# Two input copies moved behind the state's high and low parts in a pipelined slot

## The chip, the core and the metric

The kernel runs on one core of a Trainium2 chip. Its engines are PE (TensorE, matrix multiplication), ACT (ScalarE), DVE (VectorE), POOL (GpSimd) and SP (SyncE, which issues DMAs here). They run side by side, each in its own program order, and wait for each other through semaphores. The metric is the device time of one execution in microseconds (us); the figure for a kernel is the median of its runs.

## The reference

For 64 batch rows, 128 channels and 2048 positions the reference applies an S4D layer: a masked causal convolution with a kernel that is a sum of 64 complex exponentials, a direct term, and the residual.

```python
dt = jnp.exp(log_dt)
A = -jnp.exp(log_A_real) + 1j * A_imag
dtA = A * dt[:, None]
Cs = Cc * (jnp.exp(dtA) - 1.0) / A
K = 2.0 * jnp.einsum('hn,hnl->hl', Cs, jnp.exp(dtA[:, :, None] * arange(L))).real
...
u_m = u * mask[:, None, :]                    # positions below the row's length
y = irfft(rfft(u_m, n=2L) * rfft(K, n=2L))[..., :L] + u_m * D[:, None]
out = x + y * mask[:, None, :]
```

## The kernel before

The convolution is computed in chunks of 256 positions. Inside a chunk it is a product with a Toeplitz matrix; between chunks it goes through a state of 64 complex numbers (128 partitions), which is carried from chunk to chunk by powers of the exponentials (`RV`). Every operand of a wide product is kept as a high part and a low part (`uhi`/`ulo`, `uoh`/`uol`, `ehi`/`elo`, `zhi`/`zlo`, `fhi`/`flo`, `thi`/`tlo`), and `three` (L1108) multiplies them in three matmuls: high by high, low by high, high by low. ACT makes the high parts by copies, DVE and POOL the low parts by a subtraction.

One **slot** is one channel. Slots 0 to 11 and 120 to 127 are written out; the 108 between them run in a hardware loop of 18 rounds of six (`groups`). A slot of channel h works on several channels at once: `here` is h, `one` is h+1, `two` is h+2 and `back` is h-1. Each engine has a `slot` function that fixes the order of its own work; nothing else orders it.

- PE (slot, L1185): `even_sums(one)` and `odd_sums(one)` write the chunk sums of channel h+1 into the PSUM bank `v` (six matmuls of 448 columns); `turn_x(two)` transposes the input of channel h+2 into `xt_even` and `xt_odd`; `toep_even`, `toep_odd` and `turn_e(two)` follow; last comes `from_state(here)`, which multiplies `zhi` and `zlo` into the outputs `y`. `even_sums` waits for `uhi`, `elo` and `ulo`, `odd_sums` for `uod` and `uol`, and `from_state` for `flo` and `zlo`.
- ACT (slot, L735): `x_odd_high(one)` copies `xt_odd` to `uoh`; `t_high(here)`, `f_high(one)` (which waits until `from_state` of h-1 is done); `turn_evens(here)` and `turn_odds(one)`, two half copies each from `v` to the buffer `room`, `turn_odds` after the signal of `odd_sums`; `x_high(two)` makes `uhi`, `x_odd(two)` copies `xt_odd` to `uod`; `z_high(here)` scales `v` into `zhi` once `odds(here)` has ended; `turn_pairs(one)`, `e_high(two)`.
- DVE (slot, L1025): two `choose(back)` put the masked result into `xall`; `odds_turned(here)`, `pairs_turned(one)`, `odds(here)`, `pairs(one)` are steps of the state scan on `mid` and `v`; `x_low(two)` makes `ulo`, `z_low(here)` makes `zlo`; `fours_turned(one)`, `e_low(two)` (`elo`), `fours(one)`, `sixth(one)`.
- POOL (slot, L560): `product`, `f_low(here)`, `odd_low(one)` (`uol`, a subtraction of 448 columns, after `uod` and `uoh`), `product`, `t_low(here)`, `difference(two)`.
- SP loads `x` three channels ahead, stores the result of h-1, and loads the Toeplitz rows.

Line 585 is the copy helper of ACT, 780 the subtraction helper of DVE, 968 the scan helper of DVE; which call a record belongs to is told by its tiles and its place. The buffers `turned` and one of the three `uod` buffers lie in the tile `room`, so those copies are listed under that name.

Of the kernel before, what the change touches and what calls it, by code (L numbers as in the profile page):

```python
# [49 lines left out]
def s4d_kernel(nc, x, length, log_dt, C, log_A_real, A_imag, D, out):  # L50
    ctx = ExitStack()
    with ctx:
# [211 lines left out]
        def e_bank(j):  # L264

            return yb[(j + 1) % 2][1][:, 0:2 * P]

        def on(g, j, d):

            return g + (j + d) // SLOTS, (j + d) % SLOTS  # L270

        def chan(g, j):
            return g * SLOTS + j
# [5 lines left out]
        def exists(g, j, d):  # L279

            return not isinstance(g, int) or 0 <= chan(g, j) + d < H
# [301 lines left out]
        def _(act):  # L583
            def copy(dst, src):
                return act.activation(dst, src, ACT.Copy)  # L585

            def x_high(g, j):
                act.wait_ge(s_tr, 2 * chan(g, j) + 1)
                copy(uhi[j % 3][:], xt[0][:]).then_inc(s_uhi, 1)

            def x_odd(g, j):
                act.wait_ge(s_tr, 2 * chan(g, j) + 2)
                copy(uod[j % 3][:], xt[1][:]).then_inc(s_uod, 1)

            def x_odd_high(g, j):
                act.wait_ge(s_tr, 2 * chan(g, j) + 2)
                if exists(g, j, -2):
                    act.wait_ge(s_in, chan(g, j) - 1)
                copy(uoh[j % 2][:], xt[1][:, 0:EVERY]).then_inc(s_uoh, 1)
# [92 lines left out]
            def k_copy(k):  # L692
                act.wait_ge(s_kfill, k + 1)
                copy(*k_part(k)).then_inc(s_ksb, 1)

            def e_high(g, j):
                act.wait_ge(s_et, chan(g, j) + 1)
                copy(ehi[j % 2][:], e_bank(j)).then_inc(s_ehi, 1)

            def f_high(g, j):  # L700
                if exists(g, j, -1):
                    act.wait_ge(s_pf, chan(g, j))
                else:
                    act.wait_ge(s_pf0, 1)
                if exists(g, j, -2):
                    act.wait_ge(s_y, 2 * chan(g, j) - 2)
                copy(fhi[j % 2][:], pf[j % 2][:, ::-1]).then_inc(s_fhi, 1)

            def t_high(g, j):
                act.wait_ge(s_t[j % 2], 16 * (chan(g, 0) // 2 + j // 2 + 1))  # L710
                copy(thi[j % 2][:], traw[j % 2][:, ::-1]).then_inc(s_thi, 1)
# [6 lines left out]
            def turn_odds(g, j):  # L718
                act.wait_ge(s_in, chan(g, j) + 1)
                turned_halves(turned[j % 2][:, 0:3], chunks(vb[j % 2])[:, 1:6:2]).then_inc(s_turn1, 1)  # L720

            def turn_pairs(g, j):
                act.wait_ge(s_pairs, chan(g, j) + 1)
                turned_halves(turned[j % 2][:, 3:5], chunks(vb[j % 2])[:, 2:5:2]).then_inc(s_turn2, 1)

            def turn_evens(g, j):
                act.wait_ge(s_evens, chan(g, j) + 1)
                turned_halves(turned[j % 2][:, 0:3], chunks(vb[j % 2])[:, 2:7:2]).then_inc(s_turn4, 1)

            def z_high(g, j):  # L730
                act.wait_ge(s_states, chan(g, j) + 1)
                act.activation(zhi[j % 2][:, B:], vb[j % 2][:, B:NC * B], ACT.Copy,
                               scale=RV[:, 6:7, chan(g, j)]).then_inc(s_zhi, 1)

            def slot(g, j):  # L735
                here, one, two = (g, j), on(g, j, 1), on(g, j, 2)
                has0, has1, has2 = exists(g, j, 0), exists(g, j, 1), exists(g, j, 2)
                if has1:
                    x_odd_high(*one)
                t_high(*here)  # L740
                if has1:
                    f_high(*one)
                turn_evens(*here)
                if has1:
                    turn_odds(*one)
                    if isinstance(g, int) and g == 0 and 1 <= j <= 4:
                        k_copy(j)
                if has2:
                    x_high(*two)
                    x_odd(*two)  # L750
                z_high(*here)
                if has1:
                    turn_pairs(*one)
                if has2:
                    e_high(*two)

            e_high(0, 0)
# [13 lines left out]
        def _(dve):  # L771
# [7 lines left out]
            def less(dst, src, high):  # L779
                return dve.tensor_tensor(dst, src, high.bitcast(F32), ALU.subtract)  # L780

            def x_low(g, j):
                dve.wait_ge(s_uhi, chan(g, j) + 1)
                return less(ulo[j % 3][:], xt[0][:], uhi[j % 3][:]).then_inc(s_ulo, 1)
# [164 lines left out]
            def e_low(g, j):  # L949
                dve.wait_ge(s_ehi, chan(g, j) + 1)  # L950
                less(elo[j % 2][:], e_bank(j), ehi[j % 2][:]).then_inc(s_elo, 1)

            def choose(g, j, part):

                a = part * 512
                dve.memset(tick[:, part:part + 1], 0.0)
                dve.copy_predicated(xs[j][:, a:a + 512], mask[:, a:a + 512], yb[j % 2][part][:]).then_inc(s_pred, 1)  # L957
# [8 lines left out]
            def times(out, src, h, k, other):  # L966

                return dve.scalar_tensor_tensor(out=out, in0=src, scalar=RV[:, k:k + 1, h], in1=other,  # L968
                                                op0=ALU.mult, op1=ALU.add)

            def pairs_turned(g, j):

                h, z, m, w = scan(g, j)
                dve.wait_ge(s_turn1, h + 1)
                times(m[:], w[:, 0:3], h, 1, z[:, 2:7:2]).then_inc(s_mid1, 1)

            def pairs(g, j):

                h, z, m, w = scan(g, j)
                dve.wait_ge(s_mid1, h + 1)  # L980
                times(z[:, 2:7:2], z[:, 1:6:2], h, 0, m[:]).then_inc(s_pairs, 1)

            def scan(g, j):

                return chan(g, j), chunks(vb[j % 2]), mid[j % 2], turned[j % 2]
# [7 lines left out]
            def fours(g, j):  # L993

                h, z, m, w = scan(g, j)
                dve.wait_ge(s_mid2, h + 1)
                times(z[:, 6:3:-2], z[:, 4:1:-2], h, 2, m[:, 1::-1]).then_inc(s_fours, 1)
# [9 lines left out]
            def odds_turned(g, j):  # L1007

                h, z, m, w = scan(g, j)
                dve.wait_ge(s_turn4, h + 1)  # L1010
                times(m[:], w[:, 0:3], h, 1, z[:, 3:8:2]).then_inc(s_mid4, 1)

            def odds(g, j):

                h, z, m, w = scan(g, j)
                dve.wait_ge(s_mid4, h + 1)
                times(z[:, 3:8:2], z[:, 2:7:2], h, 0, m[:]).then_inc(s_states, 1)

            def z_low(g, j):
                dve.wait_ge(s_zhi, chan(g, j) + 1)  # L1020
                dve.scalar_tensor_tensor(out=zlo[j % 2][:, B:], in0=vb[j % 2][:, B:NC * B], scalar=RV[:, 6:7, chan(g, j)],  # L1021
                                         in1=zhi[j % 2][:, B:].bitcast(F32), op0=ALU.mult,
                                         op1=ALU.subtract).then_inc(s_zlo, 1)

            def slot(g, j):  # L1025
                h = chan(g, j)
                here, one, two, back = (g, j), on(g, j, 1), on(g, j, 2), on(g, j, -1)
                has0, has1, has2, hasb = exists(g, j, 0), exists(g, j, 1), exists(g, j, 2), exists(g, j, -1)
                if hasb:
                    dve.wait_ge(s_y, 2 * h - 1)  # L1030
                    choose(*back, 0)
                    dve.wait_ge(s_y, 2 * h)
                    choose(*back, 1)
                odds_turned(*here)
                if has1:
                    pairs_turned(*one)
                odds(*here)
                if has1:
                    pairs(*one)
                if has2:  # L1040
                    x_low(*two)
                z_low(*here)
                if has1:
                    fours_turned(*one)
                if has2:
                    e_low(*two)
                if has1:
                    fours(*one)
                    sixth(*one)
                if isinstance(g, int) and g == 0 and j == 1:  # L1050
                    dve.wait_ge(s_ksb, 1)
                    add_d(slice(1, 5))
                if isinstance(g, int) and g == 0 and j == 4:
                    dve.wait_ge(s_ksb, 4)
                    add_d(slice(5, SQ))
# [260 lines left out]
```

## Time and profile before

| | us |
|---|---|
| median of 3 runs | 862.51 (862.41 to 863.89) |
| profiled execution | 864.69 |
| its span (first to last instruction) | 862.8 |
| mean granted clock of TensorE | 0.996 of full speed |

The page gives PE as busy for 821.8 us (95% of the span), DVE 743.1, ACT 674.4 and POOL 603.6. Matmuls are pipelined, so their records overlap and a full row does not mean that PE never waits: a wait shows in the distance between the starts of its weight loads (PEld) and matmuls. In the timelines the first column is the start in us from the span's start, the second the duration; "x4" merges four records.

### The profile page before, as it was taken

What the parts mean: (1) busy time and instruction counts of PE and PEld (TensorE: products, weight loads), DVE (VectorE), ACT (ScalarE), POOL (GpSimd) and SP (SyncE); (2) the same over time, 40 slices, a digit from 0 to 9 for tenths busy, and PEclk for the clock granted to TensorE, in tenths of its full rate; (3) what the DMA queues carried; (4) which work ended last, traced back from release to release, by engine and by line L of the source; (5) the groups of instructions that cost most, each with busy time, mean ns of one, the idle gap of its engine ahead of it and who ended that gap; (6) DMA issues with size and microseconds to landing.
All of it is one profiled execution on the core that took longest, in us unless ns stands there. A gap on an engine that the chain in (4) does not pass through costs nothing.

```text
span 862.8 us, 23096 instructions
## 1 busy us (share of the span) xinstructions
PE 821.8 (95%) x6299; PEld 787.6 (91%) x6299; DVE 743.1 (86%) x2041; ACT 674.4 (78%) x1722; POOL 603.6 (70%) x847
## 2 busy tenths in 40 slices
PE   0779999999999999999999999999999999999997
PEld 0668999999999999999999999999999999999996
DVE  7857898888888888888888888888888888888886
ACT  4667887878788887878787878888787878787874
POOL 5965767667676767677776767676767777776763
PEclk9989999999999999999999999999999999999999
DMA  4133677777676776767676767677676767676764
GB/s 106 34 84 94 185 198 185 193 178 191 188 194 188 191 191 185 193 185 193 184 190 187 195 185 193 188 192 190 186 195 181 197 181 197 181 193 186 197 186 135
DMA packets 161394, 152.73 MB, mean 177 GB/s; under 512 B 13656, under 2 KB 161240, under 8 KB 161240
## 3 DMA queue, kind: packets, MB, share of 16 engines
q1 hardware_dynamic: 161064, 152.15, 65.9%
q8 instruction: 12, 0.20, 0.1%
q10 hardware_dynamic: 304, 0.26, 0.1%
q14 instruction: 14, 0.11, 0.0%
HBM read 84.02 MB, written 67.30 MB: 175 GB/s over the span
## 4 chain that ended last, share of the span: by engine, by line
PE 88%; ACT 3%; DMA 3%; DVE 3%; SPq 1%; issue 1%; POOL 0%; DVEq 0%; ACTq 0%; POOLq 0%
PE y L1110 15%; PE y L1111 13%; PE y L1112 13%; PE y L1158 12%; PE xt_even L1095 6%; PE xt_odd L1095 6%; PE v L1110 6%; PE v L1112 6%; PE v L1111 6%; DMA xall<-in_x_dram 3%; PE y L1105 2%; PE y L1106 2%; SPq L369 1%; ACT B L585 0%; DVE zlo L1021 0%
## 5 line engine op out<-in xcount | busy, mean ns | idle before, releaser
L585 ACT ACTIVATE room<-v 64x192 f32<-64x192 f32 (+1 forms) x768 | 236.4, 308 | 27.5 <-PE v L1112 2.4
L968 DVE SCALAR_TENSOR_TENSOR mid<-room,RV,v 128x192 f32<-128x192 f32 (+2 forms) x512 | 185.1, 361 | 73.8 <-ACT room L585 55.9
L557 POOL TENSOR_TENSOR uol<-uod,uoh 128x448 fp32r<-128x448 f32 x85 | 98.4, 1158 | 139.9 <-issue 139.9
L968 DVE SCALAR_TENSOR_TENSOR v<-v,RV,mid 128x192 f32<-128x192 f32 (+2 forms) x512 | 177.7, 370 | 16.5
L1110 PE MATMUL y<-thi,uhi 128*128 128x256 f32 x511 | 186.4, 365 | 0.0
L957 DVE COPY_PREDICATED xall<-mask,y 128x512 f32<-128x512 int32 x254 | 178.2, 752 | 1.4 <-issue 1.3
L538 POOL TENSOR_TENSOR room<-W,B 128x256 f32 (+1 forms) x254 | 161.8, 637 | 23.5 <-POOL room L547 11.1
L1110 PE MATMUL y<-fhi,zhi 128*128 128x256 f32 x511 | 153.7, 301 | 3.2 <-DVE zlo L1021 3.2
L1112 PE MATMUL y<-fhi,zlo 128*128 128x256 f32 x511 | 144.2, 282 | 0.0
L1111 PE MATMUL y<-tlo,uhi 128*128 128x256 f32 x511 | 144.1, 282 | 0.0
L1111 PE MATMUL y<-flo,zhi 128*128 128x256 f32 x511 | 144.1, 282 | 0.0
L1112 PE MATMUL y<-thi,ulo 128*128 128x256 f32 x511 | 143.9, 282 | 0.0
L1158 PE MATMUL y<-traw,uod 128*128 128x128 f32 x680 | 131.2, 274 | 0.0
L1110 PEld LDWEIGHTS y<-fhi,zhi 128*128 128x128 f32 x511 | 96.6, 189 | 14.6 <-issue 4.2
L1158 PEld LDWEIGHTS y<-traw,uod 128*128 128x128 f32 x680 | 105.1, 191 | 0.0
L1111 PEld LDWEIGHTS y<-tlo,uhi 128*128 128x128 f32 x511 | 98.4, 193 | 0.0
L1110 PEld LDWEIGHTS y<-thi,uhi 128*128 128x128 f32 x511 | 98.0, 192 | 0.1
L557 POOL TENSOR_TENSOR uol<-room,uoh 128x448 fp32r<-128x448 f32 x43 | 49.7, 1157 | 68.5 <-issue 68.0
L1111 PEld LDWEIGHTS y<-flo,zhi 128*128 128x128 f32 x511 | 97.1, 190 | 0.0
L1112 PEld LDWEIGHTS y<-fhi,zlo 128*128 128x128 f32 x511 | 97.0, 190 | 0.0
L528 POOL TENSOR_TENSOR tlo<-traw,thi 128x256 fp32r<-128x256 f32 x128 | 94.6, 739 | 2.9 <-ACT thi L585 2.9
L1112 PEld LDWEIGHTS y<-thi,ulo 128*128 128x128 f32 x511 | 96.5, 189 | 0.0
(223 smaller groups left out, 1987.1 us busy)
## 6 DMA issues: line engine op xcount, KB each, us to landing
xall<-in_x_dram SPq DMA_DIRECT2D x256, 256.0 KB, 4.3
out_dram<-xall SPq DMA_DIRECT2D x254, 256.0 KB, 3.4
traw<-krows SPq DMA_DIRECT2D x128, 128.0 KB, 3.0
NXY<-B SPq DMA_DIRECT2D x2, 512.0 KB, 6.3
krows<-ksb SPq DMA_DIRECT2D x8, 1.0 KB, 2.1
krows<-ksb SPq DMA_DIRECT2D x8, 4.0 KB, 3.8
krows<-ksb SPq DMA_DIRECT2D x8, 11.0 KB, 3.8
out_dram<-xall SPq DMA_DIRECT2D x1, 128.0 KB, 2.4
```

The source lines that it names most:

```text
L528: pool.tensor_tensor(tlo[j % 2][:], traw[j % 2][:, ::-1], thi[j % 2][:].bitcast(F32), ALU.subtract).then_inc(s_tlo, 1)
L538: pool.tensor_tensor((tw1, tw2)[which], w, b, ALU.mult).then_inc(s_gpa, 1)
L557: pool.tensor_tensor(uol[j % 2][:], uod[j % 3][:, 0:EVERY], uoh[j % 2][:].bitcast(F32), ALU.subtract).then_inc(s_uol, 1)
L585: return act.activation(dst, src, ACT.Copy)
L957: dve.copy_predicated(xs[j][:, a:a + 512], mask[:, a:a + 512], yb[j % 2][part][:]).then_inc(s_pred, 1)
L968: return dve.scalar_tensor_tensor(out=out, in0=src, scalar=RV[:, k:k + 1, h], in1=other, op0=ALU.mult, op1=ALU.add)
L1095: mm = pe.transpose(xt[par][:, c * P:(c + 1) * P], xs[j][:, b * BLK:(b + 1) * BLK], ident[:])
L1105: pe.transpose(e_bank(j)[:, 0:P], pf[j % 2][:, 0:P], ident[:])
L1110: pe.matmul(o, a_hi, b_hi, start=start, stop=False, skip_group_check=True)
L1111: pe.matmul(o, a_hi, b_lo, start=False, stop=False, skip_group_check=True)
L1112: return pe.matmul(o, a_lo, b_hi, start=False, stop=stop, skip_group_check=True)
L1158: mm = pe.matmul(y_cols(g, j, c)[:, BLK:2 * BLK], uod[j % 3][:, b], traw[k][:, :BLK - 1:-1], start=False, stop=False, skip_group_check=True)
```

## The change

In ACT's slot `x_odd(two)` moves from behind `x_high(two)` to behind `turn_pairs(one)`, so that `z_high(here)` stands directly behind `x_high(two)`. In DVE's slot `x_low(two)` moves from ahead of `z_low(here)` to behind `fours_turned(one)`, and `fours(one)` now stands ahead of `e_low(two)`. Nothing is added or removed, and the instructions of PE, POOL and SP stand as before.

```diff
@@ ACT slot
                 if has2:
                     x_high(*two)
-                    x_odd(*two)
                 z_high(*here)
                 if has1:
                     turn_pairs(*one)
                 if has2:
+                    x_odd(*two)
                     e_high(*two)
@@ DVE slot
                 odds(*here)
                 if has1:
                     pairs(*one)
-                if has2:
-                    x_low(*two)
                 z_low(*here)
                 if has1:
                     fours_turned(*one)
                 if has2:
+                    x_low(*two)
+                if has1:
+                    fours(*one)
+                if has2:
                     e_low(*two)
                 if has1:
-                    fours(*one)
                     sixth(*one)
```

ACT in the loop, before, from `x_high(two)` to `x_odd_high` of the next slot. ISA and REGISTER_ALU are instructions of the sequencer that set an address or a count; here one of them, and not `zhi`, carries the wait for `s_states`, the signal of `odds`.

```order
L585 ACTIVATE uhi<-xt_even 128x512 [waits s_tr]
L592 REGISTER_ALU
L585 ACTIVATE uod<-xt_odd 128x512 [waits s_tr]
L732 ISA [waits s_states]
L732 ACTIVATE zhi<-v,RV 128x448
L585 ACTIVATE room<-v 64x128 [waits s_pairs]
L585 ACTIVATE room<-v 64x128
L697 REGISTER_ALU
L585 ACTIVATE ehi<-y 128x256 [waits s_et]
L585 ACTIVATE uoh<-xt_odd 128x448 [waits s_in,s_tr]
```

The same place of ACT in the changed kernel:

```order
L585 ACTIVATE uhi<-xt_even 128x512 [waits s_tr]
L732 ISA [waits s_states]
L732 ACTIVATE zhi<-v,RV 128x448
L585 ACTIVATE room<-v 64x128 [waits s_pairs]
L585 ACTIVATE room<-v 64x128
L592 REGISTER_ALU
L585 ACTIVATE uod<-xt_odd 128x512 [waits s_tr]
L697 REGISTER_ALU
L585 ACTIVATE ehi<-y 128x256 [waits s_et]
L585 ACTIVATE uoh<-xt_odd 128x448 [waits s_in,s_tr]
```

The copy to `uod` now stands behind the wait for `s_states` and ahead of `ehi` and `uoh`, as one instruction with its register step.

DVE in the loop, before, from `odds(here)` to `fours(one)`:

```order
L968 SCALAR_TENSOR_TENSOR v<-v,RV,mid 128x3x64 [waits s_mid4]
L968 ISA [waits s_mid1]
L968 SCALAR_TENSOR_TENSOR v<-v,RV,mid 128x3x64
L783 REGISTER_ALU
L780 TENSOR_TENSOR ulo<-xt_even,uhi 128x512 [waits s_uhi]
L1021 ISA [waits s_zhi]
L1021 SCALAR_TENSOR_TENSOR zlo<-v,RV,zhi 128x448
L968 ISA [waits s_turn2]
L968 SCALAR_TENSOR_TENSOR mid<-room,RV,v 128x128
L780 TENSOR_TENSOR elo<-y,ehi 128x256 [waits s_ehi]
L968 ISA [waits s_mid2]
L968 SCALAR_TENSOR_TENSOR v<-v,RV,mid 128x2x64
```

The same place of DVE in the changed kernel:

```order
L968 SCALAR_TENSOR_TENSOR v<-v,RV,mid 128x3x64 [waits s_mid4]
L968 ISA [waits s_mid1]
L968 SCALAR_TENSOR_TENSOR v<-v,RV,mid 128x3x64
L1021 ISA [waits s_zhi]
L1021 SCALAR_TENSOR_TENSOR zlo<-v,RV,zhi 128x448
L968 ISA [waits s_turn2]
L968 SCALAR_TENSOR_TENSOR mid<-room,RV,v 128x128
L783 REGISTER_ALU
L780 TENSOR_TENSOR ulo<-xt_even,uhi 128x512 [waits s_uhi]
L968 ISA [waits s_mid2]
L968 SCALAR_TENSOR_TENSOR v<-v,RV,mid 128x2x64
L780 TENSOR_TENSOR elo<-y,ehi 128x256 [waits s_ehi]
```

`ulo` has gone behind `zlo` and `mid`, and `elo` has two instructions (`ulo` and `v`) more ahead of it since `zlo`.

## Rows read from the trace of the kernel before

**Rows 1.** Busy us (records) of PE, PEld, DVE, ACT, POOL; then PEclk, DMA share, GB/s
```profile
75.00:83.00 8.00, 7.54 (x61) 7.21 (x60) 5.98 (x16) 5.83 (x16) 4.45 (x6) 1.00 0.54 147
```

**Rows 2.** Timeline of PE's weight loads in one slot of the loop
```profile
408.95 0.30 PEld L1158 LDWEIGHTS y<-traw,room 128*128 128x128 f32 x2
409.18 0.19 PEld L1110 LDWEIGHTS y<-thi,uhi 128*128 128x128 f32 x1
...
409.53 0.31 PEld L1158 LDWEIGHTS y<-traw,room 128*128 128x128 f32 x2
409.94 0.19 PEld L1110 LDWEIGHTS y<-fhi,zhi 128*128 128x128 f32 x1
...
411.36 0.19 PEld L1110 LDWEIGHTS v<-uhi,ehi 128*128 128x128 f32 x1
...
411.89 0.19 PEld L1110 LDWEIGHTS v<-uoh,ehi 128*128 128x128 f32 x1
```

**Rows 3.** Timeline of PE in that slot: last matmul of odd_sums
```profile
406.26 0.37 PE L1112 MATMUL v<-uoh,elo 128*128 128x448 f32 x1
```

**Rows 4.** Timeline of ACT in that slot
```profile
406.67 0.33 ACT L585 ACTIVATE room<-v 64x192 f32<-64x192 f32 x1
...
407.35 0.60 ACT L585 ACTIVATE uhi<-xt_even 128x512 fp32r<-128x512 f32 x1
407.85 0.59 ACT L585 ACTIVATE uod<-xt_odd 128x512 f32<-128x512 f32 x1
408.36 0.64 ACT L732 ACTIVATE zhi<-v,RV 128x448 fp32r<-128x448 f32 x1
409.02 0.56 ACT L585 ACTIVATE room<-v 64x128 f32<-64x128 f32 x2
409.60 0.39 ACT L585 ACTIVATE ehi<-y 128x256 fp32r<-128x256 f32 x1
409.88 0.54 ACT L585 ACTIVATE uoh<-xt_odd 128x448 fp32r<-128x448 f32 x1
```

**Rows 5.** Timeline of DVE in that slot
```profile
407.47 0.41 DVE L968 SCALAR_TENSOR_TENSOR mid<-room,RV,v 128x192 f32<-128x192 f32 x1 [0.48 <-ACT room L585]
...
407.80 0.42 DVE L968 SCALAR_TENSOR_TENSOR v<-v,RV,mid 128x192 f32<-128x192 f32 x1
...
408.46 0.68 DVE L780 TENSOR_TENSOR ulo<-xt_even,uhi 128x512 fp32r<-128x512 f32 x1
409.13 0.69 DVE L1021 SCALAR_TENSOR_TENSOR zlo<-v,RV,zhi 128x448 fp32r<-128x448 f32 x1
...
410.01 0.42 DVE L780 TENSOR_TENSOR elo<-y,ehi 128x256 fp32r<-128x256 f32 x1
```

**Rows 6.** Timeline of POOL in that slot
```profile
410.55 1.16 POOL L557 TENSOR_TENSOR uol<-uod,uoh 128x448 fp32r<-128x448 f32 x1 [1.56 <-issue]
411.67 0.66 POOL L538 TENSOR_TENSOR room<-W,B 128x256 f32 x1
```

**Rows 7.** Timeline of ACT: two zhi of the loop six slots apart, two neighbours written out
```profile
302.45 0.64 ACT L732 ACTIVATE zhi<-v,RV 128x448 fp32r<-128x448 f32 x1
...
339.84 0.64 ACT L732 ACTIVATE zhi<-v,RV 128x448 fp32r<-128x448 f32 x1
...
819.42 0.64 ACT L732 ACTIVATE zhi<-v,RV 128x448 fp32r<-128x448 f32 x1
...
825.51 0.64 ACT L732 ACTIVATE zhi<-v,RV 128x448 fp32r<-128x448 f32 x1
```

**Rows 8.** Timeline of POOL in an early slot: the low part of the odd input
```profile
77.59 1.16 POOL L557 TENSOR_TENSOR uol<-room,uoh 128x448 fp32r<-128x448 f32 x1 [3.12 <-issue]
```

**Rows 9.** Timeline of PE's weight loads: two sums that started behind a wait
```profile
52.88 0.19 PEld L1110 LDWEIGHTS v<-uhi,ehi 128*128 128x128 f32 x1 [2.17 <-issue]
...
78.87 0.19 PEld L1110 LDWEIGHTS v<-uoh,ehi 128*128 128x128 f32 x1
```

**Rows 10.** Timeline of PE: third matmul of the sum whose load stands at 52.88
```profile
53.40 0.37 PE L1112 MATMUL v<-uhi,elo 128*128 128x448 f32 x1
```

## The prediction

> **What bounds the kernel now.** I read the busy times first: the page has PE at 95%, so the question is whether PE works without a break or is paced by a ring of waits. The timeline of PE's weight loads in one slot of the loop answers it. From the two loads of L1158 to the next load PE normally needs 409.18 - 408.95 = 0.23 us; ahead of the first load of `from_state` it is 409.94 - 409.53 = 0.41 [rows 2]. So PE stands still for 0.18 us in each slot, and what ends it is `zlo`: it ends at 409.13 + 0.69 = 409.82, and the load follows 0.12 later [rows 2, 5]. A slot of the loop lasts (339.84 - 302.45) / 6 = 6.232 us, one written out 825.51 - 819.42 = 6.09 [rows 7].
>
> Next I followed the ring backwards, engine by engine. `zlo` (409.13) starts 0.13 after the end of `zhi` (408.36 + 0.64 = 409.00). `zhi` starts 0.14 after the end of `odds` on DVE (407.80 + 0.42 = 408.22). `odds` stands right behind `pairs_turned` (407.47), and this one waited for ACT's `turn_odds`, which starts at 406.67, 0.04 after the last matmul of `odd_sums` (406.26 + 0.37 = 406.63) [rows 3 to 5]. So the ring is: `odd_sums` ends, `turn_odds`, `pairs_turned`, `odds`, `zhi`, `zlo`, `from_state`, the sums of the next channel. I call the start of `turn_odds` T; T is 406.67 here, and the next one is at T + 6.23.
>
> **What the change does to `zhi` and `zlo`: next to nothing in the loop.** The change takes one copy out of ACT's queue ahead of `zhi` and one subtraction out of DVE's queue ahead of `zlo`. Whether that helps depends on what each of them waited for. ACT's queue would have let `zhi` start at 407.85 + 0.50 = 408.35, taking the distance from `uhi` to `uod` (407.35 to 407.85) as the price of such a copy [rows 4]; it did start at 408.36. But the data came at 408.22, and the 0.14 after it is the distance that also stands between `zhi` and `zlo` (0.13) [rows 4, 5]; in both places an ISA instruction carries the wait. So the signal of `odds` alone already puts `zhi` at 408.36, and with `uod` out of the way it stays there. Could it come earlier? If the 0.14 were the queue's doing and the true delay were the 0.04 of `turn_odds` [rows 3, 4], `zhi` would come 0.10 earlier. I take 0 and keep 0.10 as the other end. `zlo` is the same case: `ulo` ends at 408.46 + 0.68 = 409.14, at the very moment when `zhi`'s data are usable (409.13) [rows 5]; removing `ulo` leaves `zlo` at 409.13. Gain in the loop: 0 to 0.10 us a slot, taken as 0.
>
> **What it does to the copies behind: they come half a microsecond later.** In the changed order ACT has nothing to do between the end of `uhi` and `zhi`, and pays for `uod` later. `zhi` at 408.36, the two half copies at 409.02, and at 409.60, where `ehi` stood, now `uod`. `ehi` then starts at 409.60 + 0.50 = 410.10, `uoh` at + 0.28 (409.60 to 409.88) = 410.38, and `uoh` ends at + 0.54 = 410.92 instead of 410.42 [rows 4]. That is the whole 0.50 us, and ACT is not short of time for it; what counts is who waits.
>
> POOL's `uol` waits for both copies. It started at 410.55, 0.13 after the end of `uoh`, lasts 1.16 and ended at 411.71 [rows 4, 6]; `odd_sums` loads its first weights at 411.89 [rows 2]. How soon after `uol` PE can load is in an early slot: `uol` ends at 77.59 + 1.16 = 78.75, the load stands at 78.87, 0.12 later [rows 8, 9], as after `zlo`. So the slack was 411.89 - 411.71 - 0.12 = 0.06 us, and it is asked for 0.50. **This is the term that decides.**
>
> The ring with it, in the old slot's clock: `uol` starts at 410.92 + 0.13 = 411.05 and ends at 412.21; PE loads at 412.33. When such a sum starts from a standstill its third matmul stands 53.40 - 52.88 = 0.52 behind the load [rows 9, 10]; that gives 412.85, and `turn_odds` follows 406.67 - 406.26 = 0.41 after that start [rows 3, 4]: 413.26. Less 406.67 this is a slot of 6.59 us, against 6.23: **+0.36 us**. PE now waits at `odd_sums`, some 0.4 us.
>
> **The rest of the change.** `elo`: in its old place (410.01) now stands `ulo`, which takes up to 0.67 (408.46 to 409.13), then `fours`, a scan step shorter than the 0.33 between 407.47 and 407.80, then `elo`, 0.42: it ends by 411.43 instead of 410.43 [rows 5]. `even_sums` loads at 411.36 [rows 2], so with the 0.12 it is held up by at most 0.19 us. That is hidden, because `odd_sums` behind it can't go before 412.33; without that cover it would cost 0.19. DVE has the time: it waited 0.48 us for ACT at 407.47 [rows 5], and the later `choose` and `odds_turned` use some of that. `ulo`, 1.55 us later than before, is needed only by `even_sums` too. PE's `turn_x` waits for `uod`, `uoh` and `ulo` of an earlier channel, half a slot later: nothing. POOL's `t_low` and `difference`, queued behind `uol`, slide with it, and so do the matmuls that read them, since these stand behind `odd_sums`: nothing. No DMA is moved, and SP's waits are for results that leave several slots before their buffer is loaded again.
>
> **The sum.** Loop: 108 slots x 0.36 = 38.9 us. Written out: there the wait stands on `zhi` itself, without an ISA instruction, so `zhi` may gain up to 0.10 of the 0.50; I take 0.28 us for the 12 slots of the pace of 6.09: 3.4 us. In the first five slots `uol` decides already (78.87 is its end + 0.12 [rows 8, 9]) and ACT also copies the kernel's tables ahead of `uhi`; those copies and `uoh` are not moved in time, so 0. Last two slots: neither moved call exists. In all +42 us: 864.7 + 42 = 907 for a profiled execution, 862.5 + 42 = **904.5 us** for the median, which lies 2.2 us below the profiled execution before. Both unknowns pull downwards: `zhi` 0.10 earlier makes it 108 x 0.10 = 11 us less, and if the third matmul comes 0.44 instead of 0.52 behind its load, which is my estimate where `even_sums` has only just ended, another 9. Upwards stands a tenth of the 0.36 for rounding in six links of 0.01, and any slip of POOL behind: 5 us. That makes 885 to 910.
>
> A rule speaks on POOL's part. The Trainium skill, Perfetto Trace Analysis, GPSIMD Engine Instruction, says that a GpSimd record's duration is not to be trusted and that start-to-start spacing should be used. Spacing gives 411.67 - 410.55 = 1.12 [rows 6] in place of 1.16, 120 x 0.04 = 5 us less, so 900 by the rule. The trace speaks for the record here: PE's load follows the recorded end by 0.12, as it does after DVE's `zlo` [rows 2, 5, 8, 9].
>
> **Rivals.**
> 1. *The stall goes, and nothing takes its place (faster).* It needs `odds` to be done when `uhi` frees ACT at 407.85; then `zhi` starts 0.5 earlier, `uoh` keeps its time, and PE's 0.18 us go: 120 x 0.18 = 22 us less, 841 us. Against it: `odds` ends at 408.22, and it hangs on `turn_odds`, that is on PE's own sums [rows 3 to 5]. Break-even is the point where `zhi` starts by 0.44 (0.50 less the slack of 0.06) earlier than now. 4%.
> 2. *`uoh` is late but POOL's true end lies well ahead of its record*, so that only `elo` holds up the sums: 0.06 to 0.19 us a slot, 7 to 23 us more, 870 to 885. Against it the 0.12 of [rows 8, 9]. 7%.
> 3. *The clock falls.* PE will idle more in each slot, and the Trainium skill, TensorE: Matmul & The Clock Gate, HAM oscillation, warns that repeated PE idling can bring the lower clock. In 75 to 83 us PE left 0.46 of 8 us unused and was granted 1.00 [rows 1], about what I expect now; if the loop ran at the lower clock, PE's 6.05 us a slot (6.23 - 0.18) would double, over 600 us more. 1%.
> 4. *No change*: the delay of `uoh` is absorbed, since PE has 0.18 us to give back at `from_state`. But that stall follows `zlo`, which follows the sums, so it moves with them. 3%.
>
> **How the numbers follow.** The forecast has 85%, all of it slower; rivals 2 and 3 are slower as well. The likeliest case is 904.5 us. The range is 885 to 910: the forecast's own ends, which leave out the better part of rival 2, rivals 1, 3 and 4, together 15%. Differences under 0.2% (1.7 us) can't be told from no change here. Faster 0.04, same 0.03, slower 0.93.
>
> **What would show it.** In the changed profile: slots of the loop 6.5 to 6.6 us apart; `zhi` still 0.14 behind the end of `odds` and 1.69 behind `turn_odds`; `uod` where `ehi` stood, 1.24 behind `zhi`; `uoh` ending 2.56 behind the start of `zhi` (now 2.06); `uol` named as what PE waits for at `odd_sums`, several tenths of a us in each slot; `zlo` no earlier against `turn_odds` than now (2.46). I am wrong if `zhi` starts right behind `uhi`, if `odd_sums` loads well ahead of `uol`'s recorded end, or if a slot takes 6.2 us or less.

## The result: 900.5 us, and where the time went

| | before | after |
|---|---|---|
| median | 862.56 us (862.41 to 863.89, 4 runs) | 900.49 us (900.35 to 900.62, 4 runs) |
| profiled execution | 864.7 us | 900.6 us, span 898.8 |
| one slot of the loop | 6.23 us | 6.55 us |
| one slot written out | 6.09 us | 6.34 us |

The ratio is 1.0436, with a 95% interval of 1.0418 to 1.0454: the change costs 38 us. The clock of TensorE is no part of it: the span has a mean granted clock of 0.995 (0.996 before), and the stretch of 100 us from the middle of the loop was granted the full one. The row of this stretch, after and then before (columns: start and length, busy us and instructions of PE, PEld, DVE, ACT and POOL, granted clock, DMA share, GB/s):

```profile
430.00:530.00 100.00, 98.79 (x735) 90.50 (x734) 81.03 (x229) 78.19 (x201) 66.70 (x90) 1.00 0.67 180
```

```profile
430.00:530.00 100.00, 100.00 (x772) 96.24 (x772) 87.84 (x243) 80.55 (x208) 71.75 (x97) 1.00 0.70 189
```

A warning stands in these rows too. PE's busy time fell by 1.2% (98.79 us for 100.00), the number of its matmuls by 4.8% (735 for 772). The records overlap: in PE's rows further down a matmul is recorded with 0.36 us while the next one starts 0.20 behind it, so the first 0.16 us of a standstill don't show as idle time. The distances between starts show them.

The pace of a slot comes from two `zhi` of the same kind, six slots apart: (370.24 - 330.92) / 6 = 6.55 us. Of before it was 6.23 [rows 7]. The two rows are from ACT's timeline of the changed kernel:

```profile
330.92 0.64 ACT L732 ACTIVATE zhi<-v,RV 128x448 fp32r<-128x448 f32 x1 [0.41 <-DVE v L968]
...
370.24 0.63 ACT L732 ACTIVATE zhi<-v,RV 128x448 fp32r<-128x448 f32 x1 [0.41 <-DVE v L968]
```

One slot on ACT, from one `turn_odds` to the next. In the terms of the prediction T is 434.07:

```profile
434.07 0.66 ACT L585 ACTIVATE room<-v 64x192 f32<-64x192 f32 x2 [0.45 <-PE v L1113]
434.76 0.60 ACT L585 ACTIVATE uhi<-xt_even 128x512 fp32r<-128x512 f32 x1
435.77 0.64 ACT L732 ACTIVATE zhi<-v,RV 128x448 fp32r<-128x448 f32 x1 [0.41 <-DVE v L968]
436.43 0.55 ACT L585 ACTIVATE room<-v 64x128 f32<-64x128 f32 x2
437.01 0.60 ACT L585 ACTIVATE uod<-xt_odd 128x512 f32<-128x512 f32 x1
437.50 0.38 ACT L585 ACTIVATE ehi<-y 128x256 fp32r<-128x256 f32 x1
437.76 0.55 ACT L585 ACTIVATE uoh<-xt_odd 128x448 fp32r<-128x448 f32 x1
...
440.62 0.66 ACT L585 ACTIVATE room<-v 64x192 f32<-64x192 f32 x2 [0.43 <-PE v L1113]
```

Compare with [rows 4]. There `zhi` stood 408.36 - 406.67 = 1.69 behind T, and here it stands 1.70 behind: the copy that was taken out of its way brought it nothing. The queue now has a hole of 0.41 us ahead of `zhi`, and what ends it is DVE's `v`, which is `odds`. Behind `zhi` the copy `uod` takes the place that `ehi` had, and `uoh` comes half a microsecond later.

The same slot on POOL, then PE's weight loads, then PE's matmuls. The load with `y<-fhi,zhi` is the first one of `from_state`, that with `v<-uhi,ehi` the first one of `even_sums`, and that with `v<-uoh,ehi` the first one of `odd_sums`:

```profile
438.45 1.15 POOL L557 TENSOR_TENSOR uol<-uod,uoh 128x448 fp32r<-128x448 f32 x1 [1.91 <-ACT uod L585]
```

```profile
436.95 0.30 PEld L1159 LDWEIGHTS y<-traw,uod 128*128 128x128 f32 x2
437.35 0.19 PEld L1111 LDWEIGHTS y<-fhi,zhi 128*128 128x128 f32 x1
...
438.77 0.19 PEld L1111 LDWEIGHTS v<-uhi,ehi 128*128 128x128 f32 x1
438.89 0.19 PEld L1112 LDWEIGHTS v<-ulo,ehi 128*128 128x128 f32 x1
439.09 0.19 PEld L1113 LDWEIGHTS v<-uhi,elo 128*128 128x128 f32 x1
439.71 0.19 PEld L1111 LDWEIGHTS v<-uoh,ehi 128*128 128x128 f32 x1 [0.43 <-issue]
```

```profile
439.09 0.36 PE L1112 MATMUL v<-ulo,ehi 128*128 128x448 f32 x1
439.29 0.36 PE L1113 MATMUL v<-uhi,elo 128*128 128x448 f32 x1
439.75 0.44 PE L1111 MATMUL v<-uoh,ehi 128*128 128x448 f32 x1
...
440.22 0.36 PE L1113 MATMUL v<-uoh,elo 128*128 128x448 f32 x1
```

`uoh` ends at 437.76 + 0.55 = 438.31, `uol` starts at 438.45 and ends at 439.60, and the load follows at 439.71. The profile names `uod` as what `uol` waited for, but `uod` had ended at 437.01 + 0.60 = 437.61; it is `uoh` that ended last. In the slot of before the load of `odd_sums` stood 411.89 - 411.36 = 0.53 behind that of `even_sums` [rows 2], and here 439.71 - 438.77 = 0.94, so it comes 0.41 us late.

PE's matmuls lose a little less. A load normally stands 0.20 ahead of its matmul (438.89 and 439.09), and here only 0.04 (439.71 and 439.75). What counts is the third matmul of `odd_sums`. Before, it stood here:

```profile
412.49 0.37 PE L1112 MATMUL v<-uoh,elo 128*128 128x448 f32 x1
```

That is 412.49 - 411.36 = 1.13 behind the load of `even_sums` [rows 2], and after the change 440.22 - 438.77 = 1.45. The difference, 0.32 us, is the whole growth of the slot. The old standstill ahead of `from_state` is still there: 437.35 - 436.95 = 0.40, before 0.41 [rows 2].

The view that sums up the waits of the whole span tells the same (columns: who waited at which line, for whom: us, times, longest):

```profile
PEld v L1111 <- issue: 56.2, 126, 2.2
...
ACT zhi L732 <- DVE v L968: 48.7, 122, 1.4
```

PE's loads of `v` at L1111 now wait 56.2 us in 126 places, 0.45 us each and one for nearly every channel. The profile puts this down to "issue", that is, to nothing that it sees. Only the timeline shows that the load stands 0.11 to 0.12 us behind the end of `uol`, in 126 of the 128 channels. The last row of the fence has this counterpart in the same view of the kernel before:

```profile
ACT zhi L732 <- DVE v L968: 2.2, 2, 1.4
```

From 2 waits of 2.2 us in all it went to 122 waits of 48.7 us: the queue in front of it got empty, and the data did not get any earlier.

### The profile page after: what moved, and what is told of

It is laid out like the page before. It is cut to its first block, busy times and chain, and to the rows that moved or that the text cites. A ratio compares the mean times of both kernels' runs of the same rounds, so it can differ in the third digit from the quotient of the medians.

```text
span 898.8 us, 23096 instructions
## 1 busy us (share of the span) xinstructions
PE 850.6 (95%) x6299; PEld 779.8 (87%) x6299; DVE 719.7 (80%) x2041; ACT 683.0 (76%) x1722; POOL 601.9 (67%) x847
## 4 chain that ended last, share of the span: by engine, by line
PE 88%; ACT 3%; issue 3%; DVE 2%; DMA 2%; SPq 1%; POOL 1%; DVEq 0%; ACTq 0%; POOLq 0%
PE y L1111 15%; PE y L1113 13%; PE y L1112 13%; PE y L1159 12%; PE v L1111 9%; PE xt_even L1096 6%; PE xt_odd L1096 6%; PE v L1113 5%; PE v L1112 5%; PE y L1107 1%; PE y L1106 1%; DMA xall<-in_x_dram 1%; ACT room L585 1%; POOL uol L557 1%; ACT B L585 0%
## 5 line engine op out<-in xcount | busy, mean ns | idle before, releaser
L968 DVE SCALAR_TENSOR_TENSOR mid<-room,RV,v 128x192 f32<-128x192 f32 (+2 forms) x512 | 182.5, 356 | 66.1 <-ACT room L585 66.0
L1111 PE MATMUL y<-thi,uhi 128*128 128x256 f32 x511 | 186.4, 365 | 0.0
L1111 PE MATMUL y<-fhi,zhi 128*128 128x256 f32 x511 | 153.9, 301 | 1.4 <-DVE zlo L1021 1.4
L1021 DVE SCALAR_TENSOR_TENSOR zlo<-v,RV,zhi 128x448 fp32r<-128x448 f32 x128 | 87.5, 684 | 76.5 <-ACT zhi L732 76.5
L732 ACT ACTIVATE zhi<-v,RV 128x448 fp32r<-128x448 f32 x128 | 81.2, 635 | 48.8 <-DVE v L968 48.7
L1111 PEld LDWEIGHTS y<-fhi,zhi 128*128 128x128 f32 x511 | 96.7, 189 | 12.0 <-issue 1.7
L1111 PEld LDWEIGHTS y<-thi,uhi 128*128 128x128 f32 x511 | 98.0, 192 | 0.1
```

The source lines that it names most:

```text
L1111: pe.matmul(o, a_hi, b_hi, start=start, stop=False, skip_group_check=True)
```

## The experiments

The theory is that of the prediction: the late `uoh` makes `uol` and with it `odd_sums` late, and `zhi` gains nothing from its free queue, since `odds` comes too late for it. The rivals are that DVE's half of the change does the harm (through `elo`, or through some other slip), that POOL's `uol` has nothing to do with it, and that no order of these instructions lets `zhi` go earlier.

| what was run | median us | ratio to before, 95% |
|---|---|---|
| the whole change | 900.5 | 1.042 to 1.045 |
| ACT's half alone | 900.1 | 1.042 to 1.047 |
| DVE's half alone | 864.3 | 1.001 to 1.004 |
| change, with `uoh` first | 870.0 | 1.006 to 1.011 |
| change, with `odds` first | 847.7 | 0.982 to 0.986 |
| before, with `odds` first | 861.5 | 0.998 to 1.000 |
| ACT's half, with `odds` first | 851.0 | 0.985 to 0.990 |
| change, with `odds` and `uoh` first | 843.9 | 0.976 to 0.982 |

**ACT's half alone.** Only the copy `x_odd(*two)` moves behind `z_high(*here)`; DVE's order is that of before.

```diff
 # ACT's slot
                 if has2:
                     x_high(*two)
-                    x_odd(*two)
                 z_high(*here)
 ...
                 if has2:
+                    x_odd(*two)
                     e_high(*two)
```

> ACT's half of the change alone: x_odd(two) behind turn_pairs(one); DVE as before. Theory (uoh comes 0.5 us later, and uol with it; zhi does not come earlier because it waits for the signal of odds): the same ring as in the changed kernel, a slot of the loop of 6.55 us, 899 to 902 us. Rival (DVE's half makes the loss, by holding up elo): no loss here, 858 to 864 us.

Measured: 900.13 us (898.21 to 901.13), ratio 1.0445 (1.0424 to 1.0465). This half alone costs all that the change costs. Its timelines, of ACT and then of DVE:

```profile
432.82 0.64 ACT L732 ACTIVATE zhi<-v,RV 128x448 fp32r<-128x448 f32 x1 [0.41 <-DVE v L968]
```

```profile
432.92 0.68 DVE L780 TENSOR_TENSOR ulo<-xt_even,uhi 128x512 fp32r<-128x512 f32 x1
433.60 0.68 DVE L1021 SCALAR_TENSOR_TENSOR zlo<-v,RV,zhi 128x448 fp32r<-128x448 f32 x1
```

`turn_odds` starts at 431.13 here, so `zhi` stands 1.69 behind it and `zlo` 2.47, with `ulo` still ahead of `zlo`. Both distances are those of the kernel with the whole change. Whether `ulo` stands ahead of `zlo` or not makes no difference to `zlo` as long as `odds` is late.

**DVE's half alone.** `z_low(*here)` and `fours_turned(*one)` go ahead of the subtraction that makes `ulo`; ACT's order is that of before.

```diff
 # DVE's slot
+                z_low(*here)
+                if has1:
+                    fours_turned(*one)
                 if has2:
                     x_low(*two)
-                z_low(*here)
                 if has1:
-                    fours_turned(*one)
+                    fours(*one)
                 if has2:
                     e_low(*two)
                 if has1:
-                    fours(*one)
                     sixth(*one)
```

> DVE's half alone: x_low(two) behind fours_turned(one), fours(one) ahead of e_low(two); ACT as before. Theory: zlo starts no earlier, since it waits for zhi (0.13 after its end), and elo, which in the changed kernel ended 2.12 us after zlo's start, would let even_sums load at 4.72 us behind turn_odds where it loads at 4.69 now: +0.03 us a slot, 863 to 868 us. Rival (elo holds up the sums by the upper bound of 0.19 us): 880 us or more. Rival (DVE's half alone is a gain, because ulo was in zlo's way): under 860 us.

Measured: 864.25 us, ratio 1.0025 (1.0011 to 1.0039): 1.8 us slower, so the half isn't quite free. `zhi` (432.23) stands 1.69 behind `turn_odds` (430.54), and `zlo` 2.47 behind it, though nothing is in DVE's way any more:

```profile
433.01 0.68 DVE L1021 SCALAR_TENSOR_TENSOR zlo<-v,RV,zhi 128x448 fp32r<-128x448 f32 x1 [0.59 <-ACT zhi L732]
```

DVE now waits 0.59 us with `zlo` at the head of its queue. That this costs something can be seen at `elo`, which stands behind it (DVE's timeline, then PE's loads):

```profile
428.41 0.41 DVE L780 TENSOR_TENSOR elo<-y,ehi 128x256 fp32r<-128x256 f32 x1
```

```profile
429.01 0.19 PEld L1111 LDWEIGHTS v<-uhi,ehi 128*128 128x128 f32 x1
```

The load comes 0.19 after the end of `elo` (428.82) and 429.01 - 427.50 = 1.51 behind the first load of `from_state`; undelayed it is 411.36 - 409.94 = 1.42 [rows 2]. In the next slot it is 1.42 again, 0.09 behind the end of `elo`. Over a round of six slots `zhi` stands 6.23, 6.23, 6.30, 6.27, 6.22 and 6.24 us apart, so two slots of a round are longer, and not every slot by 0.03 as I had expected. Both lie at the end of the round. The load above belongs to the last slot of PE's round. In the trace one more instruction of the sequencer (ALU_OP) stands ahead of the load there; it starts at 428.93, and the load 0.08 behind it. In the slot after it DVE's loop branches back, and `choose` starts about a third of a microsecond later than in the others; the last section has this in another kernel.

**The change, with `uoh` made earlier.** The high copy of the odd part is taken out of the start of the next slot and put right behind `uod`, ahead of `ehi`. So `uol` has back 0.26 of the 0.50 us that `uod` took from it.

```diff
 # ACT's slot
-                if has1:
-                    x_odd_high(*one)
                 t_high(*here)
 ...
                     x_odd(*two)
+                    x_odd_high(*two)
                     e_high(*two)
 # and x_odd_high(0, 1) once, ahead of the slots
```

> The changed kernel, with x_odd_high(two) moved from the start of the next ACT slot to ahead of e_high(two): uoh comes 0.26 us earlier, ehi 0.43 later. Theory (uol's arrival sets the slot): the slot shortens by that 0.26 to 6.29, unless elo, now late, takes over at about 6.35: 868 to 877 us. Rival (the loss of 38 us lies in something else than uol's arrival, such as elo): 900 us or more, since elo comes later here.

Measured: 869.99 us, ratio 1.0082 (1.0059 to 1.0106). This gives back 900.5 - 870.0 = 30.5 of the 38 us and moves nothing else by more than one copy. (`room` is the buffer of `uod` in the program's names.) In this kernel POOL and PE read:

```profile
437.48 1.16 POOL L557 TENSOR_TENSOR uol<-room,uoh 128x448 fp32r<-128x448 f32 x1 [1.74 <-ACT room L585]
```

```profile
438.75 0.19 PEld L1111 LDWEIGHTS v<-uoh,ehi 128*128 128x128 f32 x1
```

`uol` ends at 438.64 and the load stands 0.11 behind it. PE still waits for `uol`, only for less. The other part of the remaining time is `elo`, now pushed back by `uoh` on ACT (DVE's timeline, then PE's loads):

```profile
437.66 0.42 DVE L780 TENSOR_TENSOR elo<-y,ehi 128x256 fp32r<-128x256 f32 x1
```

```profile
436.65 0.19 PEld L1111 LDWEIGHTS y<-fhi,zhi 128*128 128x128 f32 x1
...
438.15 0.19 PEld L1111 LDWEIGHTS v<-uhi,ehi 128*128 128x128 f32 x1
```

`elo` ends at 438.08, when the load is just due (436.65 + 1.42 = 438.07), and the load comes 0.07 behind its end: 0.08 late. In the last slot of PE's round it is 0.19 late (`elo` ends at 431.67, the load stands at 431.86), with the same extra instruction ahead of it as with DVE's half alone. The prediction had up to 0.19 for `elo` without cover, as 0.07 for its end and 0.12 for the signal; in five slots of six it is 0.01 and 0.07. The slots are (340.22 - 302.25) / 6 = 6.33 us apart.

**The change, with `odds` made earlier.** Now the other side. The prediction's first rival (the stall goes, and nothing takes its place) needs `odds` to be done when `uhi` frees ACT. In DVE's queue `pairs_turned` of the next channel stands ahead of `odds`. Its results aren't needed by `odds`, so the two can be swapped.

```diff
 # DVE's slot
                 odds_turned(*here)
+                odds(*here)
                 if has1:
                     pairs_turned(*one)
-                odds(*here)
-                if has1:
                     pairs(*one)
```

> The changed kernel, and on DVE odds(here) stands ahead of pairs_turned(one), so that the signal zhi waits for no longer hangs on turn_odds of this slot. Theory (the only thing missing was that odds is done when uhi frees ACT): odds ends by about 0.85 us behind turn_odds, zhi starts right behind uhi (1.2 behind turn_odds instead of 1.7), uoh is back at its time of before, PE's stall ahead of from_state goes, and what is left is the ring through uoh and uol of about 6.08 us a slot: 843 to 850 us. Rival (the later copies are a loss wherever zhi stands): 890 or more. Rival (DVE becomes the bound, its scan steps now wait for each other): 860 to 880 us.

Measured: 847.68 us, ratio 0.9839 (0.9817 to 0.9860). DVE and ACT of this kernel:

```profile
433.41 0.43 DVE L968 SCALAR_TENSOR_TENSOR v<-v,RV,mid 128x192 f32<-128x192 f32 x1
...
435.06 0.68 DVE L1021 SCALAR_TENSOR_TENSOR zlo<-v,RV,zhi 128x448 fp32r<-128x448 f32 x1 [0.17 <-ACT zhi L732]
```

```profile
433.11 0.66 ACT L585 ACTIVATE room<-v 64x192 f32<-64x192 f32 x2 [0.34 <-PE v L1112]
433.79 0.60 ACT L585 ACTIVATE uhi<-xt_even 128x512 fp32r<-128x512 f32 x1
434.29 0.63 ACT L732 ACTIVATE zhi<-v,RV 128x448 fp32r<-128x448 f32 x1
```

`odds` ends at 433.84, before ACT is free, so `zhi` goes right behind `uhi`: 1.18 behind T instead of 1.70. `uod`, `ehi` and `uoh` stand behind it at the distances that they have after the change (`uoh` starts 436.28 - 434.29 = 1.99 behind `zhi`, as 437.76 - 435.77), and so the chain from T to `uol` is shorter by the 0.52. All 38 us of loss and 15 us more are gone. The load of `odd_sums` still stands 0.11 behind the end of `uol`, but in five slots of six it is in time for its matmul, which starts 0.20 behind the one before it; in the sixth it starts 0.36 behind. The mean slot, (440.35 - 403.77) / 6 = 6.10 us, is close to the 6.05 that the prediction gave PE for its own work.

**Before, with `odds` made earlier.** The same swap of DVE's two calls, in the kernel before.

> The kernel before, with only odds(here) ahead of pairs_turned(one) on DVE. Theory (zhi has two things in its way in the old kernel, the signal of odds and ACT's copy to uod, each of which alone holds it at 1.69 us behind turn_odds): taking away one of them gives next to nothing, 0.02 us a slot, 857 to 863 us. Rival (the signal of odds was the whole matter, and the change is not needed for the gain): 846 to 850 us.

Measured: 861.49 us, ratio 0.9992 (0.9980 to 1.0004): no difference. ACT in this kernel:

```profile
412.48 0.60 ACT L585 ACTIVATE uhi<-xt_even 128x512 fp32r<-128x512 f32 x1
412.98 0.59 ACT L585 ACTIVATE room<-xt_odd 128x512 f32<-128x512 f32 x1
413.45 0.64 ACT L732 ACTIVATE zhi<-v,RV 128x448 fp32r<-128x448 f32 x1
```

`odds` ends at 412.17 + 0.43 = 412.60, and `zhi` starts 0.85 after that. Now it is the copy `uod` (here under the name `room`) that holds it, as `odds` held it in the changed kernel. Either cause alone is enough, so taking away only one of them shows nothing. This run and the changed kernel together show both.

**ACT's half, with `odds` made earlier.** This tells what DVE's half of the change is worth once `odds` is early.

> ACT's half of the change and odds(here) ahead of pairs_turned(one); on DVE x_low(two) stays ahead of z_low(here). Theory: zhi starts at 1.2 us behind turn_odds, but zlo now stands behind ulo at about 2.33 (instead of 2.46 in the kernel before and about 1.97 with both halves), so most of PE's stall ahead of from_state goes and the slot is about 6.10 us: 848 to 853 us, 1 to 5 us over the version with DVE's half. Rival (DVE's half is needed for any gain): 858 or more. Rival (DVE's half is worth nothing): the same as that version, 845 to 849.

Measured: 851.03 us, ratio 0.9875 (0.9847 to 0.9902). DVE's order of before puts `ulo` ahead of `zlo`:

```profile
414.75 0.68 DVE L780 TENSOR_TENSOR ulo<-xt_even,uhi 128x512 fp32r<-128x512 f32 x1
415.34 0.68 DVE L1021 SCALAR_TENSOR_TENSOR zlo<-v,RV,zhi 128x448 fp32r<-128x448 f32 x1
```

`zhi` starts at 414.23, so `zlo` is 1.11 behind it, against 435.06 - 434.29 = 0.77 with the whole change. The medians differ by 851.03 - 847.68 = 3.4 us, less than a tenth of 0.34 in each slot. PE's own work covers the rest: as a mean of the rounds, five of its slots take 6.06 to 6.10 us in this version too, and only the one at the end of the round takes 6.45 against 6.28, which is 18 x 0.17 = 3.1 us. The intervals of the two ratios overlap (between 0.9847 and 0.9860), and the two were measured on different chips. But all four runs of this version (850.91 to 851.32) are slower than all four of the other (845.40 to 849.28), and the slots agree, so the 3 us are likely, though small.

**Both moves on top of the change.** `odds` first on DVE and `uoh` right behind `uod` on ACT.

> The whole change, odds(here) ahead of pairs_turned(one), and x_odd_high(two) ahead of e_high(two), so that uol comes 0.26 us earlier than in the version with odds first alone. Theory (there uol is what PE still waits for in part of the slots, 6.03 to 6.19 us a slot): PE's own work of about 6.05 us a slot is the floor, 840 to 846 us. Rival (uol no longer matters there, and elo, now later, costs something): 847 to 852 us.

Measured: 843.86 us (842.96 to 844.28), ratio 0.9790 (0.9762 to 0.9817). This is the fastest of all versions, 18 us under the kernel before. A slot lasts (440.46 - 404.01) / 6 = 6.075 us. One slot on DVE, on POOL and in PE's loads:

```profile
410.86 0.69 DVE L1021 SCALAR_TENSOR_TENSOR zlo<-v,RV,zhi 128x448 fp32r<-128x448 f32 x1 [0.17 <-ACT zhi L732]
```

```profile
412.48 1.15 POOL L557 TENSOR_TENSOR uol<-uod,uoh 128x448 fp32r<-128x448 f32 x1 [1.34 <-ACT uod L585]
```

```profile
412.01 0.19 PEld L1110 LDWEIGHTS y<-fhi,zhi 128*128 128x128 f32 x1
...
413.97 0.19 PEld L1110 LDWEIGHTS v<-uoh,ehi 128*128 128x128 f32 x1
```

`zlo` ends at 411.55, 0.46 ahead of the load that needs it, and `uol` at 413.63, 0.34 ahead. PE waits for neither, and such a slot takes 6.07 us. So this, and not the prediction's 6.05 (6.23 less the 0.18 of standing still), is what PE's own work comes to. Only in 22 of the 128 channels does the load still stand right behind `uol`.

## Why the prediction was right, point by point

The links of the ring, as the prediction put them and as the changed kernel has them:

| link | predicted | measured |
|---|---|---|
| T to `zhi` | 1.69 | 1.70 |
| `zhi` to `uod` | 1.24 | 1.24 |
| `uod` to `ehi` | 0.50 | 0.49 |
| `ehi` to `uoh` | 0.28 | 0.26 |
| length of `uoh` | 0.54 | 0.55 |
| to the start of `uol` | 0.13 | 0.14 |
| length of `uol` | 1.16 | 1.15 |
| to PE's load | 0.12 | 0.11 |
| load to third matmul | 0.52 | 0.51 |
| third matmul to next T | 0.41 | 0.40 |
| slot | 6.59 | 6.55 |

1. **`zhi` gains nothing in the loop: right.** It waits 0.41 us with its queue empty, and starts 0.14 after `odds`. The 0.10 that I had kept as the other end is 0. The swap of `odds` shows that this was the point that the sign hung on: with `odds` ending 433.84 - 433.11 = 0.73 behind T instead of 435.63 - 434.07 = 1.56, `zhi` comes 0.52 earlier and the same change is 1.6% faster than before.
2. **`uoh` comes 0.50 later, and the slack at `odd_sums` is only 0.06: right.** It starts 437.76 - 434.07 = 3.69 behind T, before 409.88 - 406.67 = 3.21 [rows 4], so 0.48 later. ACT's half alone costs everything, and making `uoh` earlier gives back four fifths.
3. **`uol` is what PE waits for: right as a mechanism, wrong in how it would show.** I said that the profile would name `uol` at `odd_sums`. It says "issue" for this wait, in 126 places, and the name has to be found from the times.
4. **`zlo` no earlier: right.** It starts at 436.55, 2.48 behind T, as before 2.46, and waits for `zhi` instead of standing behind `ulo`.
5. **`elo` up to 0.19 late, and hidden: right.** In the changed kernel it ends at 438.26 + 0.41 = 438.67, and `even_sums` loads at 438.77, which is 1.42 behind `from_state` (437.35), as without any delay. Where the cover was gone, with `uoh` first, it was 0.08 in five slots of six and 0.19 in the last of the round. DVE's half alone pays at the end of the round only: 1.8 us.
6. **The first slots: as said.** `zhi` of the early slots stands 82.59 - 74.99 = 7.60 us apart after the change, and 7.65 before.
7. **The sum was 4 us too high.** By the slots it should read 108 x 0.32 = 34.6 and 12 x 0.25 = 3.0, in all 37.6; the medians give 37.9. I had 108 x 0.36 and 12 x 0.28. The mis-sized term is the slot of the loop, 6.59 for 6.55, and it was no single error: six of the ten links were 0.01 to 0.02 too long, three 0.01 too short. I had allowed for rounding in the links, but upwards only, where it turned out downwards, and as a tenth of 0.36, though six links of 0.01 are 0.06. The 0.04 lies within that.

What the sum said about both unknowns (`zhi` 0.10 earlier, the third matmul 0.44 behind its load) turned out at the end that I took. The price of the rival with `zhi` right behind `uhi`, 841 us, was also close: once its condition holds, the kernel takes 847.7, and 843.9 when `uoh` is out of the way as well. `uoh` did keep its time (436.28 - 433.11 = 3.17 behind T, before 3.21). What that price left out is the longer slot at the end of each round, 4 us (the last section has it), and 0.02 us a slot by which PE's own work was set too low, 2 us.

## What to carry to other kernels

Moving an instruction out of the way of another gains only what the queue costs beyond the other's data: put the end of the queue's work and the arrival of the data side by side first (here 408.35 and 408.36), and if they are equal, both must be moved or neither. An instruction that is put behind one which waits for data costs all that follows it in that queue its full length, so look for the first consumer with little slack among them; here it had 0.06 us for 0.50. And look for the slack on an engine that you don't touch, by distances between instructions and not by busy shares.

## What the runs showed of the hardware that I had not expected

**Two delays for the same signal.** In the loop `zhi` starts 0.14 after the end of `odds` (435.21 + 0.42 = 435.63, and 435.77). In the slots that are written out it is 0.03:

```profile
867.06 0.42 DVE L968 SCALAR_TENSOR_TENSOR v<-v,RV,mid 128x192 f32<-128x192 f32 x1
```

```profile
867.51 0.64 ACT L732 ACTIVATE zhi<-v,RV 128x448 fp32r<-128x448 f32 x1 [0.20 <-DVE v L968]
```

The end is 867.48 and the start 867.51. The operation and the tiles are the same. What differs is that in the loop the wait is carried by an instruction of its own ahead of `zhi`. The records of line 732 on ACT's sequencer (ACTq) show it 108 times, once for each slot of the loop, while `zhi` itself is recorded 128 times (number of records, ns, first and last start):

```profile
L732 ACTq FUSED_REGOPS  x108: 46/51/51, 140.8 to 842.1; - x108
```

In the slot read above it starts at 435.66, so 0.03 behind the end of `odds` like the written-out `zhi`, and `zhi` starts 0.11 behind it. Of the 6.55 - 6.34 = 0.21 us by which the written-out slots are shorter this can be 0.11. No experiment took that instruction away in the loop, so the times fit it as the cause and don't prove it.

**GpSimd's recorded end could be used.** PE's load stood 0.11 behind the recorded end of `uol` in the changed kernel, 0.11 with `uoh` first, and 0.12 before [rows 8, 9]. The length measured after the change is 1.15 us. The Trainium skill, Perfetto Trace Analysis, GPSIMD Engine Instruction, warns against trusting such durations; for this operation the trace doesn't agree, since a consumer on another engine follows the recorded end as closely as one follows DVE's `zlo` (0.12). That the sum by spacing, 900 us, comes nearer to the measured 900.5 than my 904.5 is chance: the links of the table, with the recorded 1.15 among them, add up to the measured slot.

**One slot in six is longer, where the loop branches back.** In the changed kernel with `odds` first PE's slots take 6.06 us at five places of the round and 6.28 at the sixth, as means of the rounds; in the kernel before with `odds` first it is 6.20 and 6.32. Over 18 rounds that is 4 and 2 us. DVE's timeline of the changed kernel with `odds` first, at the longer slot and at the next one:

```profile
425.18 0.29 DVE L968 SCALAR_TENSOR_TENSOR v<-v,RV,mid 128x64 f32<-128x64 f32 x1
...
425.72 1.42 DVE L957 COPY_PREDICATED xall<-mask,y 128x512 f32<-128x512 int32 x2
...
431.48 0.29 DVE L968 SCALAR_TENSOR_TENSOR v<-v,RV,mid 128x64 f32<-128x64 f32 x1
431.69 0.74 DVE L957 COPY_PREDICATED xall<-mask,y 128x512 f32<-128x512 int32 x1
```

`choose` starts 0.54 behind the last scan step instead of 0.21. In this gap stands the branch of DVE's loop (line 258, at 425.27), which comes once in a round. `odds` of this slot then ends at 428.00, `zhi` has to wait for it again and starts at 428.13, `uol` ends at 432.08, PE's load stands at 432.20, and its matmul is the one that starts 0.36 instead of 0.20 behind its neighbour. The first slots behind the loop, written out and without a branch, take 6.06 us. No experiment moved the branch, so that it is the cause is read from its place alone.
